# Copying half of the transposed attention weights on VectorE in the last two batches of a four-stage transformer kernel

## The reference

```python
def _L0_attn_ref(x, Wq, bq, Wk, bk, Wv, bv, Wo, bo, rel_key):   # x is the normed input
    q, k, v = split_heads(x @ Wq + bq), split_heads(x @ Wk + bk), split_heads(x @ Wv + bv)
    scores = jnp.einsum('bhid,bhjd->bhij', q, k)
    rel = jnp.einsum('bhid,pd->bhip', q, rel_key)
    bias = jnp.take_along_axis(rel, ..., axis=3)                 # clip(j - i + 255, 0, 255)
    logits = jnp.where(causal, (scores + bias) * scale, -jnp.inf)
    attn = jax.nn.softmax(logits, axis=-1)
    out = jnp.einsum('bhij,bhjd->bhid', attn, v)
    return out.transpose(0, 2, 1, 3).reshape(b, s, e) @ Wo + bo

x = x + _layernorm(_L0_attn_ref(_layernorm(x), ...))   # causal, 16 heads of 8
x = x + _layernorm(_L0_ffn_ref(_layernorm(x), ...))    # gated, hidden 384
x = x + _layernorm(_L1_attn_ref(_layernorm(x), ...))   # quaternion, not causal
x = x + _layernorm(_L1_ffn_ref(_layernorm(x), ...))    # 8 experts, 2 per token
```

## Time and profile before

| | |
|---|---|
| median of 3 runs | 947.34 us (944.28 to 949.73) |
| the profiled execution | 946.77 us |
| its span | 944.7 us |
| TensorE (PE) busy | 764.6 us, 81% |
| ScalarE (ACT) busy | 495.8 us, 52% |
| VectorE (DVE) busy | 449.9 us, 48% |
| GpSimd (POOL) busy | 178.9 us, 19% |
| causal attention of batch 2 | about 265 to 413 us of the span |
| causal attention of batch 3 | about 413 to 566 us |

### The profile page before, as it was taken

The page is one execution under the profiler, slowest core; times in us unless marked ns, Lnnn a source line. Parts: engine busy times, 40 slices in busy tenths (PEclk is TensorE's granted clock), DMA queues, the critical chain, the costliest instruction groups (busy, mean ns, idle before and its releaser), DMA issues.

```text
span 944.7 us, 21455 instructions
## 1 busy us (share of the span) xinstructions
PE 764.6 (81%) x8384; PEld 548.1 (58%) x8384; DVE 449.9 (48%) x1528; ACT 495.8 (52%) x1013; POOL 178.9 (19%) x306
## 2 busy tenths in 40 slices
PE   1677888798987899988999987678786787489994
PEld 0466777576765576675565753255553563267773
DVE  3154543665545364435345552474765535521416
ACT  0335555457754659765658753548554554233321
POOL 4200101000010000010000003033324382115411
PEclk9999999899997999998999998989998998879998
DMA  3500110001300001200000410110411120011011
GB/s 99 178 2 2 68 61 2 1 3 45 114 2 12 1 13 48 89 25 12 2 13 2 130 31 20 44 29 26 154 46 45 42 61 23 6 29 46 23 34 37
DMA packets 36440, 38.29 MB, mean 41 GB/s; under 512 B 8982, under 2 KB 26220, under 8 KB 36212
## 3 DMA queue, kind: packets, MB, share of 16 engines
q1 hardware_dynamic: 34548, 33.65, 11.8%
q0 software_dynamic: 1536, 3.15, 1.1%
q10 hardware_dynamic: 256, 0.13, 0.0%
HBM read 19.87 MB, written 16.91 MB: 39 GB/s over the span
## 4 chain that ended last, share of the span: by engine, by line
PE 54%; DVE 17%; issue 14%; ACT 10%; ACTq 1%; another core or an unknown queue 1%; DMA 1%; POOL 1%; SPq 1%; POOLq 0%; DVEq 0%
PE ps L1696 5%; PE ps L1545 5%; PE ps L1566 4%; PE ps L1711 4%; PE ps L1771 4%; PE ps L1473 3%; PE ps L1579 3%; PE ps L1548 3%; PE ps L1783 3%; ACT late L908 3%; ACT probsT L758 3%; PE ps L1542 2%; PE ps L1646 2%; PE ps L1794 2%; DVE stats L1017 2%
## 5 line engine op out<-in xcount | busy, mean ns | idle before, releaser
L908 ACT ACTIVATE late<-ps,j_bias 128x512 f32<-128x512 f32 x256 | 174.7, 694 | 152.6 <-PE ps L1696 131.3
L1171 DVE TENSOR_REDUCE neg_max<-ps 128x2 f32<-128x32 f32 (+31 forms) x128 | 90.5, 707 | 166.7 <-PE ps L1551 161.5
L1696 PE MATMUL ps<-q_heads,k_parts 128*128 128x512 f32 x256 | 135.1, 542 | 20.4 <-ACT late L908 17.6
L758 ACT ACTIVATE probsT<-ps 128x128 f32<-128x128 f32 (+3 forms) x256 | 98.1, 438 | 81.0 <-PE ps L1566 67.3
L834 ACT ACTIVATE probs<-ps,neg_max 128x16 f32<-128x16 f32 (+31 forms) x256 | 110.5, 495 | 32.2 <-DVE neg_max L1171 32.2
L627 POOL TENSOR_TENSOR q_wide<-qT,eighth_mask 128x1024 f32<-128x1024 f32 x16 | 31.2, 1950 | 368.4 <-PE ps L1551 285.7
L1566 PE MATMUL ps<-ident,probs 128*128 128x128 f32 x640 | 95.6, 280 | 2.1 <-ACT probs L834 2.1
L1696 PEld LDWEIGHTS ps<-q_heads,k_parts 128*128 128x128 f32 x256 | 49.8, 200 | 72.3 <-ACT late L908 47.5
L1545 PE MATMUL ps<-kT_two,q_wide 64*64 64x262 f32 (+16 forms) x1024 | 72.7, 347 | 15.8 <-ACT probsT L758 10.3
L1566 PEld LDWEIGHTS ps<-ident,probs 128*128 128x128 f32 x640 | 74.9, 142 | 18.2 <-issue 8.2
L1711 PE MATMUL ps<-late,v_two 128*9 128x512 f32 x512 | 73.0, 636 | 9.5 <-DVE late L1157 8.3
(11 more groups left out here) (265 smaller groups left out, 1245.7 us busy)
## 6 DMA issues: line engine op xcount, KB each, us to landing
k_parts<-k_half SPq DMA_DIRECT2D x16, 256.0 KB, 3.3
q_parts<-q_half SPq DMA_DIRECT2D x16, 256.0 KB, 3.5
k_parts<-k_parts SPq DMA_DIRECT2D x16, 256.0 KB, 3.1
q_heads<-q_parts SPq DMA_DIRECT2D x64, 64.0 KB, 2.1
x_by_expert<-q_heads SPq DMA_DIRECT2D x3, 960.0 KB, 7.6
probsT<-x_by_expert SPq DMA_DIRECT2D x45, 64.0 KB
y_by_expert<-probsT SPq DMA_DIRECT2D x45, 64.0 KB
late<-in_L_ffn_w_dram SPq DMA_DIRECT2D x1, 2048.0 KB
```

What stands on the lines that cost most here:

```text
L758: return nc.scalar.activation(o, i, ACT.Copy)
L908: nc.scalar.activation(head_probs[:, i % SLOTS, :], ps[:, banks[i % len(banks)], :], ACT.Exp, bias=j_bias[:]).then_inc(e2_ready.sem, 1)
L1171: nc.vector.tensor_reduce(neg_max[:, n % 4, :], ps[:, k:k + OCT, 0:QS * (n + 1)], axis=AXX, op=ALU.max, negate=True).then_inc(max_ready.se ...
L1696: mm(ps[:, banks[i % R], :], k_parts[:, hg, kc * P:(kc + 1) * P], q_heads[:, hg % 2, g, :], start=True, stop=True).then_inc(s2_ready.sem, 1)
```

## The change

In batches 2 and 3 ScalarE no longer copies octet 0's transposed weights. VectorE does it, at the head of its slot 2n + 1, that is, behind all that it has in slot 2n (`maxima(n + 1)` and the other stages' pieces) and ahead of `copy_outT`, `divide_tile` and the other pieces of slot 2n + 1. `copy_pT` brings its waits with it: for the transposes of octet 0 of step n, and in steps 0, 8, 16 and 24 for the weighing of values that last read `probsT`. Batches 0 and 1 stay as they are.

```diff
@@ -838,7 +838,8 @@
                 yield
                 for n in range(NST):
                     yield
-                    copy_pT(act, copy, 0, pT_first, b, n)
+                    if b < 2:
+                        copy_pT(act, copy, 0, pT_first, b, n)
                     copy_pT(act, copy, 1, pT_second, b, n)
                     if n + 1 < NST:
                         exps(n + 1)
@@ -1177,6 +1178,8 @@
                     if n + 1 < NST:
                         maxima(n + 1)
                     yield
+                    if b >= 2:
+                        copy_pT(dve, copy, 0, pT_first, b, n)
                     if n >= SPT and n % SPT == 0:
                         copy_outT(b, n // SPT - 1)
                     if n >= SPT and n % SPT == 1:
```

## The result

The change makes the kernel slower: 960.61 us (median of 4 runs, 955.23 to 963.38) against 946.40 us (4 runs on the same chip), a ratio of 1.014 with a 95% interval of 1.0084 to 1.0196. The profiled execution took 955.23 us, with a span of 953.0 us and a mean granted clock of 0.944; the kernel before has 946.8, 944.7 and 0.949. The profiled execution of the changed kernel is the fastest of its four, so the two profiles are 8.3 us apart where the medians are 14.2. Lines after the edit stand a little further down: the causal scores are L1545, L1548, L1551 and L1554 (before L1542 to L1551), the transposes L1569, VectorE's copy L985, `turn` L1429, the ScalarE-gated matmul L1699.

A forecast was written before the change was run, and what follows sets the result against it. The prediction took TensorE's fixed instruction order as the bound. It summed -3 us removed, +19.7 us of late scores and +2 us of clock to +18.7 us on 946.8 us, 965 us, with a range of 953 to 978.

The forecast's parts named there:

- The bound: In batches 2 and 3, TensorE's fixed instruction order sets the time; ScalarE's lighter load is worth nothing in itself.
- The price of a copy: VectorE's copies from PSUM take 0.29, 0.42, 0.56 and 0.69 us for c = 1 to 4, nothing extra for strided output.
- What it removes: TensorE's idle time behind ScalarE's copies, ahead of `scores(n + 2)`: 3 of 5.8 us go, bounds 0 and 5.8.
- What it adds: `scores(n + 2)` starts later where VectorE is not yet free for its copy: 19.7 us over the listed places.
- the hand-over: From the end of VectorE's copy to the start of the waiting scores matmul: 0.14 us.
- Rival 1: Lateness is absorbed as VectorE catches up; if two thirds go, +4 us, 951 us, no change; 12%.
- the chain's shift by step 16's copy: Batch 2, step 17: step 16's copy moves `outT` and the unbroken chain up to `xn` by 0.95 us.
- Batch 2's steps 4 and 5: Scores behind the `xn` tiles in batch 2, step 5, with step 4's copy: +0.3 us, or +2.1 if the stall stays.
- L1034's stall: Batch 2's VectorE operation (L1033 before) took 1.95 us beside GpSimd's L627; 1.79 us of it goes.
- Batch 3's steps 5 and 6: Scores wait for the `xn` chain and step 5's copy, so `turn` ends later: +2.2 us.
- The clock: New TensorE idle times bring one more spell at the lower clock: +2 us, bounds 0 and 10 us.
- Rival 3: The clock pays most: three or more new spells at the lower level, +27 us, 974 us; 18%.

The follow-up runs named there:

- experiment 4: Kernel before, but in batches 2 and 3 ScalarE copies only 8 columns of octet 0's transposed weights, the rest left out: 935.68 us, ratio 0.9959 to the kernel before.
- experiment 1: Changed kernel with VectorE copying octet 0 only in the 42 steps where it was in time, ScalarE in the rest: 935.84 us, ratio 0.9973 to the kernel before.
- experiment 2: Changed kernel with VectorE copying octet 0 only in the 22 steps where it was late, ScalarE in the rest: 957.71 us, ratio 1.0164 to the kernel before.
- experiment 6: Changed kernel with VectorE copying octet 0 only in nine steps behind a root or the `xn` tiles: 950.85 us, ratio 1.0135 to the kernel before.
- experiment 10: Changed kernel with VectorE copying octet 0 only in the six steps with the gated product L1202 ahead: 948.16 us, ratio 1.0020 to the kernel before.
- experiment 7: Changed kernel with the octets exchanged in all 64 steps, VectorE copying octet 1 and ScalarE octet 0: 955.19 us, ratio 1.0194 to the kernel before.
- experiment 9: Changed kernel with an unused maximum over the same bank and columns ahead of each of VectorE's 64 copies: 970.77 us, ratio 1.0268 to the kernel before.

## Why the prediction was right

The side and the mechanism were right, and the size a third too high: +18.7 us forecast, +14.2 between the medians. 960.61 us lies inside the range of 953 to 978; by ratio, 2.0% was forecast and 1.4% (0.8 to 2.0) and 1.55% (1.1 to 2.0) measured in the two sets of runs. Lateness was priced 4.9 us too high and the gain 0.8 us too high, and what the clock takes differs by 1.7 us between two profiles of the changed kernel, so part of the closeness is luck. Point by point:

**The bound.** That TensorE's fixed order sets the time held. ScalarE's busy time fell by 18.4 us and the kernel became slower. No rival about a balance of loads has anything in the runs for it.

**The price of a copy** was exact, 0.29 to 0.69 us by the line drawn through the earlier trace rows. In the profile VectorE's copy takes 0.288 us at 128 columns against ScalarE's 0.276, and 0.686 at 512 against 0.595. The Trainium skill (Perfetto Trace Analysis, section Optimizing Scalar/DVE Operations) gives VectorE about 0.07 us more of fixed time on PSUM than ScalarE, as engine-busy time, and says that the profiled latency is about twice the overhead it gives. The difference of 0.01 us at 128 columns does not agree with that.

**What it removes.** 3 us were taken of at most 5.8; the changed kernel shows 2.2, the 42 steps by themselves 2.7, and with nearly all of the copy gone some 4 (the 4.3 us of experiment 4 less what its clock spells give). The choice of the middle was right. The idle time behind L758 fell to 1.6 us, as written.

**What it adds** was the right list with too high prices: 14.8 us, not 19.7. Experiments 1, 2, 6 and 10 show that all of it is in the places named and that those places cost nearly the same whether the others change or not. Two errors explain the difference. First, the hand-over. The forecast put the copy behind the full record of its predecessor and took 0.14 us from copy to scores. VectorE's copy starts some 0.08 us ahead of the recorded end. And the 0.14 us belong to the wait for octet 1's copy, which the earlier trace rows show, while it is octet 0's that now comes last; its wait takes 0.05 us (experiment 7). That makes 0.17 us less at each place, as in step 9's 0.42 against 0.59 us. In the 15 places of the list that is some 2.5 us. Second, what the next step regains. The forecast subtracted idle time of the kernel before only where `turn` waited for `xn`. But TensorE also waited for `q_rel` behind batch 2's step 17 (0.4 us) and batch 3's step 18 (0.4 us), in `turn` behind batch 2's step 25 (0.5 us, not subtracted there), and for a copy behind batch 3's step 28 (1.1 us). These idle times vanish or shrink when the step ahead is late. The steps behind regain 0.70, 0.65, 0.80 and 1.61 us (of which the forecast had 0.7), 3 us more than foreseen. Rival 1, the lateness absorbed, is true in this part, 3 of 19.7 us and not the two thirds that it needed.

Single terms: the chain's shift by step 16's copy was 0.75 us (experiment 1), not 0.95. Batch 2's steps 4 and 5 cost some 0.4 us where 0.3 were forecast, and L1034's stall of 1.79 us went as foreseen. Batch 3's steps 5 and 6 were the one place clearly under-priced, 2.7 against 2.2 us: the hand-over takes 0.26 us there (experiment 7), and they hold a clock spell of their own at 444.3 us, which no run here takes away.

**The clock** was costed at +2 us for one spell more. The shape was right, the balance was not in this execution. Two new spells stand behind the new idle times of 2.5 and 2.8 us and cost 1.6 and 1.4 us; each of these is the difference between executions with and without the spell at the same place. The forecast had spells of 7 to 10 us; these are 3.4 us long. At 263 us there is one more (+1.3 us) behind an idle time of 1.4 us that the kernel before has too, and has without a spell. On the other side the spell at the 3.5 us of idle time in step 5 was 6.8 us instead of 10.2 (-2.1), and the kernel before had its 6.8 us at 442.5 (-2.7). That gives -0.5 us in this profile. In the second it is +1.2: the spells at 265.9, 351.3 and 508.3 us cost 1.4, 1.6 and 1.6 us, and -2.0 and -1.35 us stand against them. The runs' median is 14 us over the kernel before where lateness and gain make 12.6, which leaves some 1.6 us for the clock; this last number is a difference of two noisy ones. Here the Trainium skill (TensorE: Matmul & The Clock Gate, section What's actually happening) says that the clock follows how busy TensorE has lately been, and the spells behind the new idle times agree with it. But the idle time does not decide it. The spell at 263 us, which all executions here show but that of the kernel before and those of experiments 9 and 10 (experiment 4 too has it, in which VectorE copies nothing), and the one at 557 us come and go between executions with the same idle time, and in experiment 7 an idle time of 2.7 us at batch 2's step 17 has no spell behind it: its granted clock is 1.00 from 346 to 358 us.

**Rival 3** (three spells more, 974 us) has its spells but not its price: a spell of 3.4 us costs 1.3 to 1.6 us, where the rival had 10 us for three, and they also fall away elsewhere.

**What stays open:** why the spells at 263, 349, 442, 508 and 557 us are in some executions and not in others. No kernel was run on the clock by itself.

## What to carry to other kernels

Before work is moved to a half-idle engine, read for each place at what time that engine has finished what stands ahead in its order, and what waits for it: here 9 of 64 copies made more than half of the loss and 42 made a small gain. A choice by step, with 18 copies of batch 0 beside the 42 (0.9945, 0.9918 to 0.9972), was faster than the old kernel and than the rule for all steps. When pricing a late place, subtract the idle time that the waiting engine already had in the step behind it, and take the hand-over time from the wait that will end last. In a trace of one execution compare step by step and look at the granted clock of each stretch before calling a difference a cause.

## What the runs showed of the hardware that was not expected

- On VectorE these copies start before the record of their predecessor ends: 307.03 against 306.42 + 0.69 = 307.11, 554.87 against 554.95, 340.13 against 340.22. The Trainium skill (Perfetto Trace Analysis, section Optimizing Scalar/DVE Operations) says that the write-acknowledgement half of an instruction's profiled latency overlaps with the next instruction. That there is an overlap the trace confirms, with 0.08 to 0.09 us.
- From the end of a copy to the matmul that waits for it were 0.05 to 0.06 us or 0.14 to 0.15 us, by which of two awaited semaphores came last and not by the engine that made the copy (experiment 7, both engines in both places).
- The stall of a 128x4 VectorE operation, 1.95 us beside a GpSimd operation of 1.95 us, hangs on whether the two meet: a shift of 4 us took it away, and in experiments 1 and 10, without that shift, it was there again (1.80 and 1.96 us). It stood in a chain for which TensorE waited 3.63 us.
- TensorE's spells at 1.2 GHz in the stretch came to 17.1 us before and to 20.5 and 23.9 us in two executions of the changed kernel, to 30.7 us in experiment 2 and to 10.2 us in experiment 10, with six copies moved. The two executions of the changed kernel differ in the stretch by 1.8 us, nearly all of it for that.
